# Moving the opening work of a state-space block between VectorE, GpSimd and ScalarE, and reordering the first feed-forward products

## The chip, the core and the metric

The kernel runs on one core of a Trainium2 chip. The metric is the device time of one launch in microseconds (us). TensorE (PE) multiplies and writes PSUM; VectorE (DVE), ScalarE (ACT) and GpSimd (POOL) do the elementwise work; SyncE (SP) issues the DMA transfers. Each engine works through its own list in order, and the lists are tied together by semaphores.

## The reference, cut to what matters

```python
def reference(u, W_in, conv_w, conv_b, dt_bias, A_log, D, norm_w, W_out, W_up, W_gate, W_down):
    x = u                                                  # (2, 2048, 512)
    x = _layernorm(x + attn(x, ...))
    x = _layernorm(x + ffn(x, ternary(W_up), ternary(W_gate), ternary(W_down)))
    return x

def attn(u):
    zxbcdt = einsum('bld,ed->ble', u, W_in)                # z, x, B, C, dt
    dt = softplus(zxbcdt[..., -8:] + dt_bias)
    xBC = silu(causal_conv4(xBC, conv_w, conv_b))
    dA = dt * A;  cum = cumsum(dA)                         # decays within chunks of the sequence
    y = within-chunk product (C B^T * decay) (x dt)  +  C * carried state * exp(cum)  +  x * D
    yg = y * silu(z)
    return einsum('ble,de->bld', yg * rsqrt(mean(yg^2) + eps) * norm_w, W_out)

def ternary(w):                                            # scale = mean(|W|)
    return clip(round(w / scale), -1, 1) * scale

def ffn(x):
    return einsum(silu(x Wu^T) * (x Wg^T), Wd)
```

## The kernel before

The 4096 tokens go in 8 blocks of 512 (`NB`), each block as 8 heads in four pairs (`p` = 0 to 3). Then the feed-forward part runs over the same 8 blocks in 8 slices (`q`) each; its up and gate products are done by seven products per slice instead of eight (`product`, `FACTORS`). Every weight and activation is used as a float16 high part and a float16 low part (`w_hi`, `w_lo`, `split_u`, `x_high`, `x_low`).

What a block does: `head_tile` multiplies one head's x or z columns (12 matmuls into one of three ring banks); `conv_in`, `conv`, `conv_tanh`, `silu` turn the x tile into `x_ch`; `z_tanh`, `z_gate` the z tile into `z_ch`; `cb_tile`, `cb_conv`, `cb_silu` make B and C (`b_ch`, `c_ch`) of the next block; `dt_first`, `dt_second`, `dt_ln`, `dt_third` its step sizes `dts` and `da`. `turn_x` transposes x, `x_dt` scales it, `decays` and `within` make the masked decay matrix `seg`, `states` and `state_update` the chunk states, and `outputs` the result. `skip` adds x times D into `y_ch`, `gate` multiplies by z into `yg`, `gated` and `y_low` split that, `chunk_out` multiplies by W_out. A ring bank is given to the next tile only when its x, z or B/C has been read (`ring_room`).

The order on each engine is written out by hand. Block 0 begins with a straight list (pair 1 of block 0), and `step(0, 0)` goes on with pairs 2 and 3. Into this opening is woven what is done once:

- The input weight comes in six pieces (`PIECES`); ACT makes the high part, DVE the low part. Piece 3 (columns of heads 2 and 3) is split by DVE in two halves (`w_lo_head(2)`, `w_lo_head(3)`), the last piece (heads 6 and 7) by `w_lo(5)`. Where the raw piece 5 lay, `y_hi` is written later, so the first `gated` of block 0 waits for `w_lo(5)`.
- W_out comes in two halves through the buffer `rows`. For each, POOL scales it by the norm weight (`wout_scale`), ACT makes the high part (`wout_hi`), POOL the low part (`wout_low`).
- For the ternary scales, 24 tiles of the feed-forward weights pass through two buffers of `quant`: ACT sums the magnitudes of the even ones, DVE of the odd ones (`magnitude(i)`). `load_abs(i)` waits until tile `i - 2` is summed. All of SP's transfers stand in one queue of issues: one that waits holds up all behind it.

`load_cum(n, par, p)` of SP brings the cumulative decays of a pair and waits for the `decays` that read the buffer before (`relu_ok`).

## Time and profile before

| | us |
|---|---|
| median of 3 runs | 1405.49 |
| lowest and highest | 1405.03, 1407.62 |
| the profiled execution | 1405.99 |
| its span, first to last instruction | 1404.2 |
| PE busy in the span | 1362.4 |
| DVE, ACT, POOL busy in the span | 1070.9, 802.1, 649.9 |
| mean granted TensorE clock | 0.993 |

PE is busy 97% of the span, so a time is won or lost where PE sits idle, or where its clock is granted at half. How to read it: the table of waits names who ended PE's idle stretches; the timeline of one engine gives start and length of each instruction, merged when like ones follow each other, with the idle time ahead of it in brackets.

### The profile page before, as it was taken

The page shows a single profiled execution, that of the slowest core. Times are in us where ns is not written, and L with a number is a line of the kernel's source. Part 1 is how long each engine was busy: PE and PEld are TensorE (multiplying, and loading weights), DVE is VectorE, ACT ScalarE, POOL GpSimd, SP SyncE. Part 2 cuts the span into 40 slices and gives each one's busy share as a digit, 9 for nine tenths or more (in the row PEclk, how much of TensorE's full clock was granted, in tenths as well). Part 3 has the DMA queues.
Part 4 walks back from the last instruction along what each step waited for, and adds up shares of the span by engine and source line. Part 5 has one row for each costly group of instructions (what it writes and reads, how often), then busy time and mean ns, then how long its engine had stood idle before and what let it go on. Part 6 is the DMA issues. An engine that isn't in the chain of part 4 may idle for free.

```text
span 1404.2 us, 27260 instructions
## 1 busy us (share of the span) xinstructions
PE 1362.4 (97%) x9574; PEld 888.9 (63%) x9574; DVE 1070.9 (76%) x1848; ACT 802.1 (57%) x1593; POOL 649.9 (46%) x628
## 2 busy tenths in 40 slices
PE   8899999999999999999999999999999999999998
PEld 4455555555555555556556777777777777777774
DVE  7887877886877879878775887767776767777775
ACT  6686574773856828748565555555455545545441
POOL 0574264673663736625355544434343434434331
PEclk9899999999999999999999999999999999999999
DMA  8436334263342532424325130111101010110002
GB/s 258 160 125 212 127 106 105 80 171 87 105 128 84 164 108 84 143 91 136 124 87 196 61 106 16 47 45 46 34 28 61 31 63 16 59 33 31 31 24 68
DMA packets 101342, 129.16 MB, mean 92 GB/s; under 512 B 40401, under 2 KB 61265, under 8 KB 100049
## 3 DMA queue, kind: packets, MB, share of 16 engines
q1 hardware_dynamic: 101200, 127.35, 29.3%
q8 instruction: 80, 1.31, 0.4%
q14 instruction: 62, 0.50, 0.1%
HBM read 99.93 MB, written 27.39 MB: 91 GB/s over the span
## 4 chain that ended last, share of the span: by engine, by line
PE 60%; issue 13%; DVE 12%; ACT 8%; POOL 6%; DMA 1%; ACTq 0%; POOLq 0%; SPq 0%; DVEq 0%
PE ring L1110 15%; PE p_turn L1090 8%; PE p_y L1090 7%; PE ring L873 7%; PE p_seg L1090 6%; PE p_st L1090 5%; PE ring L902 5%; DVE acc L1806 2%; ACT p_seg L1333 2%; ACT xdt L1324 2%; PE p_y L946 2%; PE p_y L954 2%; DVE seg L1904 1%; POOL sq_sum L1634 1%; DVE st L1918 1%
## 5 line engine op out<-in xcount | busy, mean ns | idle before, releaser
L873 PE MATMUL ring<-u_split,weights 128*128 128x512 f16 x1620 | 376.2, 382 | 2.1 <-DVE x_ch L1811 1.9
L873 PEld LDWEIGHTS ring<-u_split,weights 128*128 128x128 f16 x1620 | 155.6, 99 | 172.2 <-issue 8.0
L1717 POOL TENSOR_TENSOR xdt<-xdt 128x512 f32<-128x512 f32 x64 | 100.2, 1566 | 351.8 <-DVE xdt L2160 351.8
L1806 DVE SCALAR_TENSOR_TENSOR acc<-ring,taps,acc 128x511 f32<-128x511 f32 (+2 forms) x192 | 143.7, 749 | 4.5
L902 PE MATMUL ring<-w_out,raw 128*128 128x512 f16 x672 | 147.1, 379 | 0.0
L1324 ACT ACTIVATE xdt<-p_turn,dts 128x128 f32<-128x128 f32 x256 | 73.0, 376 | 84.9 <-PE p_turn L926 84.9
L1626 POOL TENSOR_TENSOR raw<-yg,raw 128x512 f16<-128x512 f32 x64 | 78.7, 1230 | 79.2 <-ACT raw L1354 78.6
L902 PEld LDWEIGHTS ring<-w_out,raw 128*128 128x128 f16 x672 | 65.7, 98 | 77.8
L1621 POOL TENSOR_TENSOR yg<-y_ch,z_ch 128x512 f32<-128x512 f32 x64 | 81.9, 1280 | 44.1 <-DVE y_ch L1926 44.1
L1333 ACT ACTIVATE p_seg<-cum_rows,cum 128x128 f32<-128x128 f32 x256 | 80.8, 388 | 6.2 <-DVE seg L1904 6.2
L1277 ACT ACTIVATE ring<-acc 128x512 f32<-128x512 f32 x64 | 38.5, 602 | 80.0 <-DVE acc L1806 79.6
L946 PE MATMUL p_y<-seg,xdt 128*128 128x128 f32 x512 | 69.9, 281 | 14.7 <-DVE seg L1904 14.2
L946 PEld LDWEIGHTS p_y<-seg,xdt 128*128 128x128 f32 x512 | 64.2, 191 | 24.4 <-DVE seg L1904 20.1
L1597 POOL TENSOR_TENSOR rstd<-var_e,exponent 128x1 f32<-128x1 f32 x32 | 20.4, 638 | 125.6 <-DVE var_e L1948 125.6
L1634 POOL TENSOR_TENSOR sq_sum<-sq_sum,sq 128x512 f32<-128x512 f32 x56 | 71.1, 1270 | 0.0
L1522 ACT ACTIVATE cum_g<-c_dec,tanh_scale 128x512 f32<-128x512 f32 x32 | 23.1, 722 | 77.6 <-DVE b_dec L2152 77.6
L1522 ACT ACTIVATE cum_g<-b_dec,tanh_scale 128x512 f32<-128x512 f32 x32 | 23.1, 722 | 71.7 <-DVE c_dec L2152 71.2
L1904 DVE TENSOR_TENSOR seg<-p_seg,cb_mask 128x512 f32<-128x512 f32 x64 | 43.9, 686 | 22.1 <-ACT p_seg L1337 22.0
L2152 DVE TENSOR_TENSOR xdt<-grow,p_turn 128x512 f32<-128x512 f32 x64 | 44.0, 687 | 17.1 <-ACT grow L1513 11.5
L1811 DVE SCALAR_TENSOR_TENSOR x_ch<-ring,acc 128x512 f32<-128x512 f32 x64 | 44.1, 689 | 15.8 <-ACT ring L1277 14.9
L2152 DVE TENSOR_TENSOR c_dec<-cum_g,p_turn 128x512 f32<-128x512 f32 x32 | 22.0, 688 | 44.1 <-PE p_turn L1090 44.1
L1522 ACT ACTIVATE grow<-xdt,tanh_scale 128x512 f32<-128x512 f32 x64 | 46.0, 719 | 14.5 <-DVE xdt L2152 13.9
(420 smaller groups left out, 3367.7 us busy)
## 6 DMA issues: line engine op xcount, KB each, us to landing
cum_rows<-cum_dram SPq DMA_DIRECT2D x64, 256.0 KB, 4.1
quant<-in_w_ffn SPq DMA_DIRECT2D x24, 512.0 KB, 4.4
quant<-in_w_ffn SPq DMA_DIRECT2D x48, 256.0 KB, 4.1
cum_g<-cum_dram SPq DMA_DIRECT2D x64, 128.0 KB, 4.4
rows<-in_u_tok SPq DMA_DIRECT2D x32, 256.0 KB, 3.7
x_dram<-rows SPq DMA_DIRECT2D x32, 256.0 KB, 2.0
tern_ug<-quant SPq DMA_DIRECT2D x32, 256.0 KB, 3.5
u_raw<-in_u_t SPq DMA_DIRECT2D x7, 1024.0 KB, 8.4
```

The source lines that it names most:

```text
L873: mm = pe.matmul(bank_k[:, :], w_in[:, ws, k, col:col + P], us[:, par, k * T:(k + 1) * T], start=(i == 0), stop=(i == 3 * KD - 1))
L902: mm = pe.matmul(ring[b][:, :], ys[:, h, c * P:(c + 1) * P], w_out[:, ws, h, :], start=(h == 0 and ys is y_hi and ws == 0), stop=(h == H - ...
L946: pe.matmul(p_y[q][:, c * P:(c + 1) * P], xdt[:, q, c, :], seg[:, q, c, :], start=(c == 0), stop=False, skip_group_check=True)
L1090: mm = pe.matmul(bank_j[:, w * 256:(w + 1) * 256], factor(weight, w, k, q), xs[par][i][:, k, :], start=(first and w == 0 and k == 0 and xs ...
L1110: mm = pe.matmul(p_down[c % 2][:, :], hidden_tile(par, m, low)[:, c * P:(c + 1) * P], t_down(m), start=(e == 0 and m == 0 and not low), st ...
L1324: ins = act.activation(xdt[:, q, c, :], p_turn[:, c * P:(c + 1) * P], ACT.Copy, scale=dts[:, owner, c, h:h + 1])
L1333: ins = act.activation(p_seg[:, c * P:(c + 1) * P], cum_b[:, (2 * p - 2 + q) % 4, c, :], ACT.Relu, bias=cum[:, owner, h, c:c + 1], scale=-1.0)
L1522: act.activation(th[second], up, ACT.Tanh, scale=tanh_scale[:, 0:1]).then_inc(tanh_ok, 1)
L1621: pool.tensor_tensor(yg[:, q, :], y_ch[:, q, :], z_ch[:, k % 4, :], ALU.mult).then_inc(yg_ok, 1)
L1634: pool.tensor_tensor(sq_sum[:, :], sq_sum[:, :], sq[:, q, :], ALU.add).then_inc(sqsum_ok, 1)
L1717: pool.tensor_tensor(tile_[:, 1, :, :], tile_[:, 0, :, :], tile_[:, 1, :, :], ALU.mult).then_inc(hid_ok, 1)
L1806: dve.scalar_tensor_tensor(acc[:, buf, k + 1:T], own[:, 0:T - 1 - k], taps[:, h, 2 - k:3 - k], acc[:, buf, k + 1:T], ALU.mult, ALU.add).th ...
```

## The change

Seven moves, five of them around the first two blocks and two at the feed-forward part:

1. Piece 3 of the input weight is split by POOL, not DVE. Each half is two instructions there (a scaling in place, then a subtraction); they stand first in POOL's list. PE waits for them by `w_half_ok`, and SP's first `load_abs` too.
2. `cb_silu` makes B before C, and `turn_b` waits for B alone; `cb` waits for all three. This holds in all blocks.
3. In pair 2 of block 0 DVE takes `skip` (both heads) and the carry in front of `cb_conv` and `dt_second` of block 1, then `within` of both heads and the state updates in front of the next convolution. `w_lo(5)` comes after `silu(4)`, and `magnitude(3)` behind `silu(5)`, next to `magnitude(5)`. On ACT `cb_tanh` stands ahead of `decays` of the second head.
4. The second half of W_out (`wout_hi(1)`, `wout_low(1)`) and ACT's `magnitude(8)` move from pair 3 of block 0 to pair 0 of block 1.
5. SP issues tiles 10 and 11 behind `load_cum(1, ·, 1)` and `load_u(2)` of block 1.
6. Opening of the feed-forward part: PE does product 5 ahead of product 6; ACT reads product 7 ahead of the last two `gated`.
7. The last block's `rms` on POOL and its `residual(NB-1, 0)` on DVE stand earlier in slice 2.

```diff
 def head_weights(h):
-    return 1 + h if h < 2 else 2 + h // 2
+    return 2 + h if h < 2 else 2 + h // 2
...
+        def act_rows(n, p, when):
+            if when == 2 and is_at(n, 0) and p == 3:
+                return None
+            return 8 if when == 0 and is_at(n, 1) and p == 0 else abs_rows(n, p, when)
...
@@ SP, step(0, 0), pair 0
-                        sp.wait_ge(w_lo_ok, 4)
+                        sp.wait_ge(w_lo_ok, 3)
+                        sp.wait_ge(w_half_ok, 2)
...
                     if is_at(n, 0) and p == 3:
                         load_abs(8)
                         load_abs(9)
+                    if is_at(n, 1) and p == 0:
+                        load_cum(n, par, 1)
+                        load_u(2)
                         load_abs(10)
                         load_abs(11)
-                    if is_at(n, 1) and p == 0:
                         load_abs(12)
                         load_abs(13)
-                        load_cum(n, par, 1)
-                        load_u(2)
...
@@ PE
             def turn_b(n, use):
-                wait_apart(pe, bc_ok, n * 3 + 3, passed["pe"])
+                wait_apart(pe, bc_ok, n * 3 + 1, passed["pe"])
...
             def cb(n, par, use):
                 pe.wait_ge(turn_free, use)
+                wait_apart(pe, bc_ok, n * 3 + 3, passed["pe"])
...
             product(0, 0, 0, 1, True)
+            pe.wait_ge(turn_free, turn_use(NB, "x01") + 1)
+            product(0, 0, 0, 5, True)
             pe.wait_ge(s1_ok, 1)
             product(0, 0, 0, 6, False)
-            pe.wait_ge(turn_free, turn_use(NB, "x01") + 1)
-            product(0, 0, 0, 5, True)
             outputs(NB, 0, 0)
...
@@ ACT, step
                     if state_slot(n, p):
                         x_dt(n, par, p, 1)
+                        if is_at(n, 0) and p == 2:
+                            cb_tanh(1, ring[ring_bank("cb", 0)])
                         decays(n, par, p, 1)
-                    if is_at(n, 0) and p == 2:
-                        cb_tanh(1, ring[ring_bank("cb", 0)])
...
+                    if is_at(n, 1) and p == 0:
+                        wout_hi(1)
                     if not end:
                         conv_tanh(n, 2 * p + 1)
...
-                    if is_at(n, 0) and p == 3:
-                        wout_hi(1)
...
             gated(NB, 0, 1)
+            chain_read(0, 0, u3, prod[7], u3_ok, c21_ok)
             act.wait_ge(scales_ok, 3)
             gated(NB, 1, 0)
             gated(NB, 1, 1)
...
@@ POOL
+            def w_lo_head(h):
+                own = raw_piece(3)[:, :, 2 * P * (h - 2):2 * P * (h - 1)]
+                pool.wait_ge(w_hi_ok, 4)
+                pool.tensor_scalar(own, own, SW, None, ALU.mult).then_inc(w_mul_ok, 1)
+                pool.wait_ge(w_mul_ok, h - 1)
+                pool.tensor_tensor(w_in[:, 1, :, 2 * P * h:2 * P * (h + 1)], own, w_in[:, 0, :, 2 * P * h:2 * P * (h + 1)],
+                                   ALU.subtract).then_inc(w_half_ok, 1)
...
+            w_lo_head(2)
+            w_lo_head(3)
             b_decay(0, 0, 0, turn_use(0, "b0"))
...
-                    if is_at(n, 0):
-                        wout_scale(1) if p == 2 else wout_low(1)
+                    if is_at(n, 0) and p == 2:
+                        wout_scale(1)
                     if p == 0 and more(n) and not is_at(n, 0):
                         corrections(n + 1, 1 - par)
+                    if is_at(n, 1) and p == 0:
+                        wout_low(1)
...
@@ DVE
             cum_turned(0, turn_use(0, "cumt0"))
-            w_lo_head(2, w_half_ok)
             cb_silu(0, 0, p_y[0])
             z_gate(0, 0)
-            w_lo_head(3, w_lo_ok)
             b_read(0, 0, turn_use(0, "b0"))
...
             w_lo(4)
             magnitude(1)
-            w_lo(5)
-            cb_conv(1, 1, ring[ring_bank("cb", 0)])
-            dt_second(1)
...
+                    if first and p == 2:
+                        cb_conv(1, 1, ring[ring_bank("cb", 0)])
+                        dt_second(1)
...
                     if first and p == 2:
                         cb_silu(1, 1, ring[ring_bank("cb", 0)])
-                    if abs_rows(n, p, 0) is not None:
+                        within(n, par, p, 1)
+                        for c in range(C - 1):
+                            state_update(n, par, p, c)
+                    elif abs_rows(n, p, 0) is not None:
                         magnitude(abs_rows(n, p, 0) + 1)
...
-                    if state_slot(n, p):
+                    if first and p == 2:
+                        w_lo(5)
+                    elif state_slot(n, p):
...
+                    if first and p == 2:
+                        magnitude(abs_rows(n, p, 0) + 1)
                     if abs_rows(n, p, 2) is not None:
                         magnitude(abs_rows(n, p, 2) + 1)
...
+                    if attention_rest(t, q) == 0:
+                        residual(NB - 1, 0, p_down[0])
                     if before:
                         summed(m, k, "c12", u2, u2_ok, 5, ALU.add)
```

Three places show what the moves make of the lists. In the names, `rows` holds the raw weight piece 3, `quant` a magnitude tile, `x_ch`, `z_ch` and `y_ch` are `silu`, `z_gate` and `skip`.

DVE at the end of the straight list's first third (block 0, behind the first `silu`), before:

```order
L1811 SCALAR_TENSOR_TENSOR x_ch<-ring,acc 128x512 [waits th_ok]
L1888 COPY cum_t<-p_turn 32x128 [waits turn_full]
L1781 SCALAR_TENSOR_TENSOR weights<-rows,weights 128x4x256 [waits w_hi_ok]
L1830 SCALAR_TENSOR_TENSOR c_ch<-p_y,acc 64x512 [waits thc_ok]
L1830 SCALAR_TENSOR_TENSOR c_ch<-p_y,acc 64x512
L1832 SCALAR_TENSOR_TENSOR b_ch<-p_y,acc 64x512
L1839 SCALAR_TENSOR_TENSOR z_ch<-thz,ring 128x512 [waits thz_ok]
L1781 SCALAR_TENSOR_TENSOR weights<-rows,weights 128x4x256 [waits w_hi_ok]
```

POOL behind its constants, now:

```order
L1677 TENSOR_SCALAR rows<-rows 128x4x256 [waits w_hi_ok,made]
L1679 TENSOR_TENSOR weights<-rows,weights 128x4x256 [waits w_mul_ok]
L1677 TENSOR_SCALAR rows<-rows 128x4x256 [waits w_hi_ok]
L1679 TENSOR_TENSOR weights<-rows,weights 128x4x256 [waits w_mul_ok]
L1617 TENSOR_TENSOR b_dec<-b_tok,dec 128x4x64 [waits dec_ok,turn_free]
```

The two splits have left DVE, and four POOL instructions now run from the moment the fourth high part is made.

DVE at the end of pair 2 of block 0, before:

```order
L1879 COPY cum<-p_turn 128x32 [waits turn_full]
L1882 TENSOR_TENSOR darg<-p_turn,cum 128x32 [waits dec_ok,cum_ok]
L1811 SCALAR_TENSOR_TENSOR x_ch<-ring,acc 128x512 [waits th_ok]
L1786 TENSOR_REDUCE abs_sum<-quant 128x1 [waits abs_in1]
L1926 SCALAR_TENSOR_TENSOR y_ch<-x_ch,d_skip,p_y 128x512 [waits yg_ok,y_full]
L1926 SCALAR_TENSOR_TENSOR y_ch<-x_ch,d_skip,p_y 128x512 [waits yg_ok]
```

and now:

```order
L1896 COPY cum<-p_turn 128x32 [waits turn_full]
L1899 TENSOR_TENSOR darg<-p_turn,cum 128x32 [waits dec_ok,cum_ok]
L1828 SCALAR_TENSOR_TENSOR x_ch<-ring,acc 128x512 [waits th_ok]
L1803 TENSOR_REDUCE abs_sum<-quant 128x1 [waits abs_in1] x2
L1943 SCALAR_TENSOR_TENSOR y_ch<-x_ch,d_skip,p_y 128x512 [waits yg_ok,y_full]
L1943 SCALAR_TENSOR_TENSOR y_ch<-x_ch,d_skip,p_y 128x512 [waits yg_ok]
```

Two magnitudes (tiles 3 and 5) stand there in a row where one stood; both use the same buffer.

SP from the magnitude tiles of pair 3 of block 0 on, before:

```order
L589 DMA quant<-in_w_ffn 128x1024 [waits abs_ok0]
L589 DMA quant<-in_w_ffn 128x1024 [waits abs_ok1]
L597 DMA cum_dram<-cum_t 32x128 [waits turn_free]
L607 DMA cum_rows<-cum_dram 128x512 [waits grow_ok,relu_ok,cumt_out]
L608 DMA cum_g<-cum_dram 64x512
L607 DMA cum_rows<-cum_dram 128x512
L608 DMA cum_g<-cum_dram 64x512
L589 DMA quant<-in_w_ffn 128x1024 [waits abs_ok0]
L589 DMA quant<-in_w_ffn 128x1024 [waits abs_ok1]
L607 DMA cum_rows<-cum_dram 128x512 [waits grow_ok,relu_ok]
L608 DMA cum_g<-cum_dram 64x512
```

and now:

```order
L614 DMA cum_rows<-cum_dram 128x512 [waits grow_ok,relu_ok]
L615 DMA cum_g<-cum_dram 64x512
L614 DMA cum_rows<-cum_dram 128x512
L615 DMA cum_g<-cum_dram 64x512
L600 DMA u_raw<-in_u_t 128x2048 [waits u_lo_ok]
L596 DMA quant<-in_w_ffn 128x1024 [waits abs_ok0]
L596 DMA quant<-in_w_ffn 128x1024 [waits abs_ok1]
L596 DMA quant<-in_w_ffn 128x1024 [waits abs_ok0]
L596 DMA quant<-in_w_ffn 128x1024 [waits abs_ok1]
```

Tiles 10 and 11 were issued ahead of the store of block 1's decays; now they are issued behind the second group of its loads and behind the next block's u.

## Rows read from the trace of the kernel before

**Rows 1.** Page, part 1: busy us (share) and instructions of each engine.
```profile
PE 1362.4 (97%) x9574; PEld 888.9 (63%) x9574; DVE 1070.9 (76%) x1848; ACT 802.1 (57%) x1593; POOL 649.9 (46%) x628
```
**Rows 2.** Waits of PE, 0 to 200 us: us in total, times, longest.
```profile
PE p_y L946 <- DVE seg L1904: 5.2, 6, 1.9
PE p_turn L911 <- DVE b_ch L1832: 3.7, 2, 3.1
PE p_st L936 <- DVE carry L1918: 2.6, 1, 2.6
```
**Rows 3.** Timeline of PE: start us, length us, line, instruction [idle before, releaser].
```profile
65.03 4.84 PE L873 MATMUL ring<-u_split,weights 128*128 128x512 f16 x12
...
97.77 0.63 PE L926 MATMUL p_turn<-ident,x_ch 128*128 128x128 f32 x4 [1.48 <-ACT xdt L1324]
...
114.47 0.60 PE L926 MATMUL p_turn<-ident,x_ch 128*128 128x128 f32 x4
```
**Rows 4.** Timeline of DVE, 18 to 23 us.
```profile
18.12 0.19 DVE L1873 TENSOR_TENSOR da<-dts,a_neg 128x32 f32<-128x32 f32 x1
18.30 0.16 DVE L1802 TENSOR_TENSOR acc<-acc,corr 128x3 f32<-128x3 f32 x1
...
22.29 1.20 DVE L1781 SCALAR_TENSOR_TENSOR weights<-rows,weights 128x1024 f16<-128x1024 f32 x1
```
**Rows 5.** Timeline of ACT: the high part of piece 3.
```profile
15.71 1.90 ACT L1249 ACTIVATE weights<-rows 128x2048 f16<-128x2048 f32 x1
```
**Rows 6.** One line of DVE: duration in ns, min/median/max, first and last start.
```profile
L1802 DVE TENSOR_TENSOR acc<-acc,corr x64: 151/678/1271, 18.3 to 733.0; 128x3 f32<-128x3 f32 x64
```
**Rows 7.** POOL: one timeline row, then durations (ns) of two lines.
```profile
1.92 0.95 POOL L1588 MEMSET carry<- 128x1024 f32 x1
...
L1669 POOL TENSOR_TENSOR rows<-rows,norm_s x8: 1041/1043/1046, 39.6 to 77.9; 128x512 f32<-128x512 f32 x8
...
L1676 POOL TENSOR_TENSOR w_out<-rows,w_out x8: 1152/1159/3199, 48.0 to 96.4; 128x512 f16<-128x512 f32 x8
```
**Rows 8.** Timeline of DVE, 53 to 87 us.
```profile
53.57 1.11 DVE L1818 TENSOR_TENSOR acc<-acc,corr 128x3 f32<-128x3 f32 x1
...
75.35 0.69 DVE L1811 SCALAR_TENSOR_TENSOR x_ch<-ring,acc 128x512 f32<-128x512 f32 x1 [0.33 <-ACT ring L1277]
75.95 1.21 DVE L1786 TENSOR_REDUCE abs_sum<-quant 128x1 f32<-128x1024 f32 x1
77.08 1.40 DVE L1926 SCALAR_TENSOR_TENSOR y_ch<-x_ch,d_skip,p_y 128x512 f32<-128x512 f32 x2
...
80.50 0.69 DVE L1904 TENSOR_TENSOR seg<-p_seg,cb_mask 128x512 f32<-128x512 f32 x1 [1.16 <-ACT p_seg L1337]
```
**Rows 9.** Timeline of SP's issues: start, length of the issue.
```profile
108.19 0.38 SPq L607 DMA_DIRECT2D cum_rows<-cum_dram  x1
...
110.23 0.96 SPq L593 DMA_DIRECT2D u_raw<-in_u_t  x1
```
**Rows 10.** DMA issues, 0 to 120 us: KB each, median us from issue to landing.
```profile
quant<-in_w_ffn SPq DMA_DIRECT2D x16, 512.0 KB, 4.7
...
rows<-in_u_tok SPq DMA_DIRECT2D x2, 256.0 KB, 10.1
```
**Rows 11.** Timeline of ACT, 92 to 103 us.
```profile
92.38 2.17 ACT L1254 ACTIVATE w_out<-rows 128x512 f16<-128x512 f32 x4
94.46 1.04 ACT L1258 ACTIVATE quant<-quant 128x1024 f32<-128x1024 f32 x1
...
100.94 1.27 ACT L1333 ACTIVATE p_seg<-cum_rows,cum 128x128 f32<-128x128 f32 x4
```
**Rows 12.** Timeline of PE, the opening of the feed-forward part.
```profile
747.06 1.05 PE L1090 MATMUL ring<-b_tok,weights 128*128 128x256 f16 x8 [0.69 <-ACT cum_g L1513]
...
757.80 1.05 PE L1090 MATMUL p_turn<-c_ch,weights 128*128 128x256 f16 x8 [1.37 <-DVE xdt L2152]
...
776.57 2.76 PE L1147 MATMUL ring<-w_out,raw 128*128 128x512 f16 x12 [0.37 <-DVE rows L1941]
```

35 lines of the change are left out of this document (16 added, 19 removed).

## The prediction, made before the result was known

> **What bounds the kernel now.** I read the page's first part first: PE is busy 97% of the span [rows 1], so only its idle stretches and its half-clock stretches can be won. The table of PE's waits over the first 200 us comes next [rows 2]. The reader should see that the large single waits are two: 2.6 us on the carry behind `skip` (L936), and 3.1 us on B of block 1 (L911). PE's timeline then shows what follows them: a tile of 12 matmuls at 65.03 takes 4.84 us where the same kind takes 2.76 at full clock [rows 3, 12], so PE ran at 1.2 instead of 2.4 GHz there. A third wait, 1.48 us at 97.77, is on ACT. In the rest of the first 130 us PE waits little, but that doesn't mean that DVE and ACT have room: they are nearly as late as PE. Last I read SP's issues and the landing times [rows 9, 10], because the change moves loads.
>
> The sum is made against the profiled execution (span 1404.2, time 1405.99) and its difference is put on the median, 1405.49. A lateness that PE carries into its long run of W_out products at the end of block 1's pair 1 passes to the end, since PE hardly waits after that.
>
> **1. Piece 3 on GpSimd.** DVE loses two instructions of 1.13 us each, start to start (22.29 in [rows 4], and one more like it), 2.3 us, in a stretch where PE waits for DVE. Unhindered that is worth 2.0 us. Now POOL's side. ACT's high part ends at 15.71 + 1.90 = 17.6 [rows 5]. No scaling of 1024 elements by a constant is in the trace. A fill of that size takes 0.95, a two-operand product of 512 takes 1.04, so 2.08 for two of them [rows 7]: the bounds. I take 1.2, near the fill, since only one operand is read. The subtraction is twice 1.16 = 2.3. Both halves are done at 17.6 + 2 × 3.5 = 24.6, the first at 21.1, earlier than DVE made it (22.29 + 1.20), so PE doesn't wait for the weights.
>
> But DVE and POOL hinder each other. The three-element addition of `conv` takes 151 ns alone and up to 1271 [rows 6], and 1.11 at 53.57 [rows 8], when POOL was in the low parts of W_out, one of which took 3.2 instead of 1.16 [rows 7] because DVE's own low part was running. All these DVE instructions read two operands from SBUF. At 18.12 and 18.30 stand two more of that kind, `da` and the first addition of `conv` [rows 4]. POOL's four instructions now start just ahead of them. `da` then waits behind the first subtraction, until 17.6 + 1.2 + 2.3 = 21.1, and the addition behind the second scaling, until 22.3: 4.0 us late, less the 2.3 given back, **+1.7** (with the bounds of the scaling +1.2 to +3.5; without hindrance −2.0). PE meets it as a wait for `da` ahead of `cum_proj` at about 18.4 and for the first `silu` later.
>
> No row shows a DVE instruction as wide as `da` held by POOL, only three-element ones. The Trainium skill, "SBUF — State Buffer", section "Who interferes with whom", says that a DVE instruction with two SBUF inputs and a GpSimd one that reads SBUF exclude each other for a whole instruction, whichever starts first. By that rule `da` is held and the sum is the one below; by the rows alone the opening could as well give −2.0, the first rival.
>
> **2. Pair 2 of block 0.** With `skip` and the carry first, `states` needs no wait, and B comes after ACT's earlier `cb_tanh`: both waits of [rows 2] go, and most of the half clock. Behind them DVE is next: `w_lo(5)` now stands in front of `dt_third` and of ACT's first `gated`, so `cum_proj` waits about 5 us for `da` of block 1. What is left, from DVE's order, is that `silu(5)` (75.35 before [rows 8]) comes about 2.0 earlier: one magnitude of 1.13 has moved behind it, and DVE's own idle time is some 1.7 shorter, less 0.8 that it waits for ACT.
>
> That gain is spent at once. `magnitude(3)` now ends at 73.9 + 1.1 = 75.0, and only then may SP issue tile 5, for the same buffer. The median from issue to landing is 4.7 [rows 10], so `magnitude(5)` runs 79.7 to 80.9, and `skip` behind it starts at 80.9 instead of 77.08 [rows 8]: **+3.8**. If the tile landed at once it would be −0.9; at the 10.1 that two other tiles took it would be +9. I take the median of its own kind. The load of the second half of W_out stands behind tile 5 in SP's queue; POOL's `wout_scale(1)` and the gates behind it come later too, which holds `z_gate(6)`: 0.5 more. Against it DVE had 1.16 idle at 80.50 [rows 8]. So `outputs` of pair 3 is 3.1 late.
>
> **3. Pair 0 of block 1.** ACT no longer does W_out (2.17) and tile 8 (1.04) at 92.38 [rows 11], which made the 1.48 wait [rows 3]. Its `z_tanh(7)` ran 2.4 behind its tile, so of the 3.1 it keeps 0.7; a tile at half clock after PE's wait costs up to 2.1 more (4.84 less 2.76), I take 1.0. `decays` of pair 0, which end at 100.94 + 1.27 = 102.2 [rows 11], are then **+1.7** late on top of item 1.
>
> **4. Tiles 10 and 11.** `load_cum(1, ·, 1)` waits for just those `decays`. Its four issues and that of u take 3.0 (108.19 to 110.23, plus 0.96 [rows 9]), so tile 10 is issued 3.0 behind them, and lands 4.7 to 10.1 later [rows 10] (its own median, and that of two transfers issued right behind the same five). I take 6.5, between them but nearer to its kind: landed at 9.5. ACT is there at 3.9 and waits 5.6; DVE waits as long for tile 11. Then ACT has `magnitude(10)` 1.1, `conv_in` and `gated` 1.7, W_out 2.1, `conv_tanh` 0.5, the wait for tile 12 (issued at 10.6, landed 15.3), `magnitude(12)` and the `z_tanh` and `growth` in front of `x_dt` 3.1: 18.4 behind `decays`. Before, PE transposed that head at 114.47 [rows 3], 12.3 behind them. **+6.1** (+4.4 with 4.7, +9.7 with 10.1). PE stands idle 5 to 6 us there, ahead of `turn_x` and the z tile of head 2.
>
> **5. B first** in all other blocks: `cb_silu` runs a pair ahead of `turn_b`, under PE's W_out products. 0. **W_out later**: its products come 15 us after the new place. 0.
>
> **6. Feed-forward opening.** Product 5 needs only `x_dt` of the second head, long done, and hides the 0.69 wait; ACT's read of product 7 ahead of two `gated` that wait for POOL ends the 1.37 wait; `rms` and `residual` earlier end the 0.37 wait [rows 12]. **−2.4**; if `outputs` or the W_out product behind them is late instead, −1.
>
> Sum: 1.7 + 1.7 + 6.1 − 2.4 = +7.1, less 0.5 for two short waits for DVE and POOL in block 1 that are there anyway: **+6.6, 1412**.
>
> **The rivals.** *No hindrance in the opening*: POOL starts a little later or DVE's small instructions slip between. Item 1 is −2.0: 1405.5 + 2.9 = 1408.4. For it: the row of a held instruction is of another shape. Against: POOL has four in a row. *The cover holds, and it gets faster*: the mechanism is the loads. If tile 5 and tile 11 land before DVE and PE need them, that is, in under 1 us and under 1.5 us beyond DVE's own work, item 2 keeps −0.9, item 3 adds the 1.48, item 6 the 2.4, and with item 1 between −2.0 and +1.7 it is 1398.7 to 1402.4; I take 1401. For it: PE has one tile of slack in its ring at each place. Against: a round trip through SP can't be shorter than a landing, and 4.7 is the median. *All prices at their upper end*: scaling 2.08 and landings of 10.1: +3.5 + 1.7 + 9.7 − 2.4 = +12.5, 1418. *The change doesn't do what it says* is no case: the lists show the moves.
>
> **The numbers.** Forecast 0.50, no hindrance 0.23, faster 0.15, upper end 0.10, the rest elsewhere. A measurement of this kernel can tell about 0.2% from no change, 2.8 us. Under 1402.7 lies most of the faster case: 0.15. From there to 1408.3: half of the second case and the forecast's low edge, 0.20. Above: 0.65. The range that leaves out 2 in 10 is 1403 to 1417: below it most of the faster case, above it most of the upper end.
>
> **What would show it.** Item 1: DVE's `da` and first `conv` addition at 1 us or more each, PE idle about 3 us at 18.4. Item 2: no wait at `states` and `turn_b` of pair 2, about 5 us at `cum_proj`, and two magnitudes on DVE with a wait for DMA of about 4 us between. Item 4: waits of ACT and DVE for `quant` DMAs near 110 us, and PE idle ahead of 120. Item 6: no idle time at the three places. Wrong would be: `da` at 0.2 us, tiles landing within 3 us, or PE busy through 115 to 123 us.

## The result, and the profile of the changed kernel

| | before | changed |
|---|---|---|
| median | 1405.49 us | 1411.82 us |
| all runs | 1404.87 to 1407.62 | 1410.27 to 1412.98 |
| profiled execution: span | 1404.2 | 1411.2 |

The ratio is 1.0041 (95% interval 1.0031 to 1.0052): the changed kernel is slower by 0.3 to 0.5%, beyond the 0.2% that can be told from no change. The forecast was 1412.0.

PE does as much as before, in a longer span (part 1 of the page: busy us, share, instructions; before it was [rows 1]):

```profile
PE 1361.0 (96%) x9574; PEld 887.5 (63%) x9574; DVE 1070.2 (76%) x1846; ACT 801.9 (57%) x1593; POOL 657.9 (47%) x632
```

So idle time was added. PE's waits from 0 to 200 us (us in total, times, longest), to be laid beside [rows 2]:

```profile
PE p_turn L935 <- ACT xdt L1333: 6.6, 1, 6.6
PE p_y L955 <- DVE seg L1921: 6.5, 4, 2.3
PE p_turn L853 <- DVE da L1890: 5.3, 3, 4.2
```

The wait of 2.6 for the carry is gone, that of 3.1 for B is down to 1.5. In their place stand 4.2 for `da` of block 1 and one of 6.6 for ACT, at a place where PE had no idle time before. Where they lie is seen on PE's timeline (start, length; in brackets the idle time before it and what ended it):

```profile
71.14 0.60 PE L853 MATMUL p_turn<-da,tri_ones 128*128 128x32 f32 x2 [4.17 <-DVE da L1890]
71.98 5.28 PE L881 MATMUL ring<-u_split,weights 128*128 128x512 f16 x12
...
124.18 1.09 PE L935 MATMUL p_turn<-ident,x_ch 128*128 128x128 f32 x4 [6.57 <-ACT xdt L1333]
125.06 4.36 PE L881 MATMUL ring<-u_split,weights 128*128 128x512 f16 x12
```

Behind both waits the tile of 12 matmuls takes 5.28 and 4.36 us instead of 2.76. The granted clock is 0.51 of full over the first of these tiles and 0.63 over the second: after it stood idle, PE ran at 1.2 instead of 2.4 GHz for the whole of the one and most of the other. That is the second part of what these waits cost. The same transposition, `turn_x` of that head, was at 114.47 before [rows 3], so PE is 9.7 us late at that point.

ACT (108.2 to 115.4 us) and DVE (109.6 to 116.7) both stood still for a transfer, and earlier DVE alone. The first two lines are the earlier place, the last two the later one:

```profile
79.46 1.22 DVE L1803 TENSOR_REDUCE abs_sum<-quant 128x1 f32<-128x1024 f32 x1 [3.56 <-DMA quant<-in_w_ffn]
80.59 1.40 DVE L1943 SCALAR_TENSOR_TENSOR y_ch<-x_ch,d_skip,p_y 128x512 f32<-128x512 f32 x2
...
115.43 1.06 ACT L1267 ACTIVATE quant<-quant 128x1024 f32<-128x1024 f32 x1 [7.24 <-DMA quant<-in_w_ffn]
...
116.66 1.22 DVE L1803 TENSOR_REDUCE abs_sum<-quant 128x1 f32<-128x1024 f32 x1 [7.08 <-DMA quant<-in_w_ffn]
```

The feed-forward opening, in PE's timeline, has none of the waits of 0.69 and 1.37 of [rows 12]. From the start of the W_out product ahead of it to the start of the one behind it are 16.7 us, before 18.8 (741.60 to 760.43):

```profile
751.13 2.76 PE L1156 MATMUL ring<-w_out,raw 128*128 128x512 f16 x12
...
767.86 2.76 PE L1156 MATMUL ring<-w_out,raw 128*128 128x512 f16 x12
```

**The lateness, place by place** (start of the same instruction, changed less before; from the two timelines). The forecast is the sum of the prediction's terms up to that place, the opening's +1.7 included:

| place | before | changed | late by | forecast |
|---|---|---|---|---|
| `outputs` of pair 0, block 0 | 47.12 | 46.13 | -1.0 | +1.7 |
| `skip` of pair 2 | 77.08 | 80.59 | +3.5 | +5.5 |
| `outputs` of pair 3, the carried part | 88.52 | 91.91 | +3.4 | +4.8 |
| end of `decays`, pair 0 of block 1 | 102.21 | 104.48 | +2.3 | +3.4 |
| `turn_x` behind tile 10 | 114.47 | 124.18 | +9.7 | +9.5 |
| first W_out products of block 1 | 129.26 | 139.36 | +10.1 | |
| W_out product ahead of the feed-forward part | 738.40 | 747.93 | +9.5 | |
| W_out product behind its opening | 760.43 | 767.86 | +7.4 | |
| end | | | +7.0 | +6.6 |

The table compares two single executions. How much the first places move between executions of the same code is seen from the traces of all the runs below: `outputs` of pair 0 starts between 45.49 and 47.71 in the ten traces with the changed opening, 46.55 on average, and at 46.45, 46.72 and 47.12 in the three with the old one. So the -1.0 of the first row is within that spread; on average the two openings are 0.2 apart.

### The profile page after: what moved, and what is told of

Same layout as the page of the kernel before. It is cut to its first block, busy times and chain, and to the rows that moved or that the text cites. A ratio compares the mean times of both kernels' runs of the same rounds, so it can differ in the third digit from the quotient of the medians.

```text
span 1411.2 us, 27276 instructions
## 1 busy us (share of the span) xinstructions
PE 1361.0 (96%) x9574; PEld 887.5 (63%) x9574; DVE 1070.2 (76%) x1846; ACT 801.9 (57%) x1593; POOL 657.9 (47%) x632
## 4 chain that ended last, share of the span: by engine, by line
PE 59%; issue 13%; DVE 12%; ACT 8%; POOL 5%; DMA 2%; SPq 0%; ACTq 0%; POOLq 0%; DVEq 0%
PE ring L1119 15%; PE p_turn L1099 7%; PE ring L881 7%; PE p_y L1099 7%; PE p_seg L1099 5%; PE p_st L1099 5%; PE ring L910 4%; DVE acc L1823 3%; ACT p_seg L1342 2%; ACT xdt L1333 2%; PE p_y L955 2%; PE p_y L963 2%; DVE seg L1921 1%; DVE st L1935 1%; POOL sq_sum L1645 1%
```

## The experiments

"Measured" gives the median, then the ratio to executions of the kernel before made together with that run (their medians lie between 1405.4 and 1405.9), with its 95% interval. Two kernels whose intervals overlap are not told apart by their times; then the traces are compared, and the text says so. `W_out at` is the start of the first W_out products of block 1 (before 129.26, changed 139.36), which sums up the first blocks without the later stretches. It is read from one execution, so a difference of about 1 us can be chance.

### Run 1: tiles 8, 10 and 11 early again

```diff
 def act_rows(n, p, when):
-    if when == 2 and is_at(n, 0) and p == 3:
-        return None
-    return 8 if when == 0 and is_at(n, 1) and p == 0 else abs_rows(n, p, when)
+    return abs_rows(n, p, when)
...
                     if is_at(n, 0) and p == 3:
                         load_abs(8)
                         load_abs(9)
+                        load_abs(10)
+                        load_abs(11)
                     if is_at(n, 1) and p == 0:
                         load_cum(n, par, 1)
                         load_u(2)
-                        load_abs(10)
-                        load_abs(11)
                         load_abs(12)
```

> Changed kernel with tiles 10 and 11 issued in pair 3 of block 0 again and ACT's magnitude of tile 8 back there; the second half of W_out stays late. Theory: PE's 6.6 us ahead of turn_x at 124.2 exist only because tile 10 is issued 3 us behind decays and lands 7 us later. Then ACT's wait of 7.2 and DVE's of 7.1 vanish, ACT's 1.1 for tile 8 is covered by its wait for z_tanh(7), and turn_x comes 12.3 to 13 behind decays instead of 19.7: about -7.4, 1404.4. Rival: the W_out high parts (2.2 us) that now stand in front of conv_tanh on ACT make most of it, together with POOL's low parts; then 3 us or more of the idle time stays and the time is 1407 to 1409.

Measured: 1409.83 us, 1.0030 [1.0017, 1.0042]; W_out at 135.97. Not 1404: the time lies just above the rival's range. The wait for tile 10 is gone, but ACT now waits for tile 12, and PE keeps 2.53 of 6.57. ACT's timeline:

```profile
111.54 2.18 ACT L1261 ACTIVATE w_out<-rows 128x512 f16<-128x512 f32 x4
114.77 0.60 ACT L1284 ACTIVATE ring<-acc 128x512 f32<-128x512 f32 x1 [1.05 <-DVE acc L1821]
117.53 1.06 ACT L1265 ACTIVATE quant<-quant 128x1024 f32<-128x1024 f32 x1 [2.16 <-DMA quant<-in_w_ffn]
```

W_out's high parts stand in front of `conv_tanh` in this run too, and ACT has to wait for DVE (1.05) behind them anyway, so they hold nothing up: the rival's mechanism falls. What stayed is again a tile issued behind `load_cum` and u: SP issued tile 12 at 109.97, and it landed 7.5 later. (The wait of 2.53 had no half clock behind it; the tile that follows took 2.75.)

### Run 2: the order of the loads alone

```diff
                     if is_at(n, 1) and p == 0:
+                        load_abs(10)
+                        load_abs(11)
                         load_cum(n, par, 1)
                         load_u(2)
-                        load_abs(10)
-                        load_abs(11)
                         load_abs(12)
```

> Changed kernel, only SP's order in pair 0 of block 1: tiles 10 and 11 ahead of the four loads of cum and of u. Theory (order of issue): tile 10 is issued right behind ACT's magnitude of tile 8, at 106.2 instead of about 107.7, and no 1 MB transfer is ahead of it, so it lands after 4.7: 110.9, ACT waits 2.8 instead of 7.2; -4.4, 1407.4. Rival (the transfers share the engines whatever the order): it lands 7.5 behind its issue again, 113.7, only -1.6, 1410.2.

Measured: 1413.06 us, 1.0051 [1.0038, 1.0065]; slower than either forecast, and by its time not told apart from the changed kernel. The profiled execution was the slowest of the five, 1417.31, and the other four lie between 1412.94 and 1413.24; W_out at 142.88 is of that one. ACT's timeline shows both tiles, with the wait ahead of each:

```profile
114.35 1.06 ACT L1267 ACTIVATE quant<-quant 128x1024 f32<-128x1024 f32 x1 [1.61 <-DMA quant<-in_w_ffn]
...
124.08 1.06 ACT L1267 ACTIVATE quant<-quant 128x1024 f32<-128x1024 f32 x1 [4.17 <-DMA quant<-in_w_ffn]
```

and SP's timeline (start and length of the issues) when they were issued:

```profile
110.72 0.81 SPq L596 DMA_DIRECT2D quant<-in_w_ffn  x2
...
113.66 0.58 SPq L600 DMA_DIRECT2D u_raw<-in_u_t  x1
115.52 1.70 SPq L596 DMA_DIRECT2D quant<-in_w_ffn  x2
```

Tile 10, ahead of u, was there 3.6 us after its issue; tile 12, behind u, 8.6 us after. So a tile is late because of what is in front of it, and not because all these loads are under way at the same time: the wait moved from one tile to the next (1.6 + 4.2 in place of 7.2). The edit itself brings 1.3 us, near the rival's 1.6: the turn ahead of tile 10's place comes 4.5 later than in the changed kernel (118.96 against 114.42), the one behind it 3.2 (127.41 against 124.18). Those 4.5 have nothing to do with the edit, since they lie in front of it. 1.6 are there at `outputs` of pair 0 already (47.71 against 46.13). The other 2.9 are half clock in pair 3 of block 0, behind a wait for `seg` of 2.94 us (2.26 in the changed kernel):

```profile
97.68 4.58 PE L881 MATMUL ring<-u_split,weights 128*128 128x512 f16 x12
```

The granted clock is 0.50 from 94 to 98 us here and 0.98 there, and the same tile took 2.76 there. That explains the profiled execution. Why the other four, at 1413, show nothing of the 1.3 to 1.6 us that the edit should bring stays open.

### Run 3: tile 3's magnitude early again

```diff
                         for c in range(C - 1):
                             state_update(n, par, p, c)
+                        magnitude(abs_rows(n, p, 0) + 1)
                     elif abs_rows(n, p, 0) is not None:
...
-                    if first and p == 2:
-                        magnitude(abs_rows(n, p, 0) + 1)
```

> Changed kernel, only DVE's magnitude of tile 3 back in front of conv of head 4, in pair 2 of block 0. Theory: DVE's wait of 3.56 us for tile 5 goes because SP can issue the tile 12 us earlier; skip starts at 77.0 to 77.5 instead of 80.6, the second half of W_out lands in time and the 0.97 wait at z_gate(6) goes too; the lateness passes unshrunk through pair 0 of block 1, since load_cum there waits for decays: -3.5, 1408.3. Rival: the 1.2 us ahead of conv pass on through silu(4), w_lo(5) and ACT's gated to the cum products, and half of the gain is lost: -1.5 to -2, 1410.

Measured: 1410.99 us, 1.0034 [1.0022, 1.0046]; W_out at 137.32, 2.0 earlier. By the times it can't be told from the changed kernel, and the profiled execution, 1413.51, is the slowest of its six; so what follows rests on the first 140 us of the traces. DVE's wait for tile 5 is gone and `skip` starts 3.6 earlier, as the theory said, but DVE then waits for ACT:

```profile
76.94 1.40 DVE L1943 SCALAR_TENSOR_TENSOR y_ch<-x_ch,d_skip,p_y 128x512 f32<-128x512 f32 x2
79.07 0.69 DVE L1856 SCALAR_TENSOR_TENSOR z_ch<-thz,ring 128x512 f32<-128x512 f32 x1 [0.48 <-ACT thz L1302]
82.36 0.69 DVE L1921 TENSOR_TENSOR seg<-p_seg,cb_mask 128x512 f32<-128x512 f32 x1 [2.60 <-ACT p_seg L1346]
```

ACT's `decays` are that late because PE's turns are, and those because `da` of block 1 now comes later still. PE's timeline:

```profile
72.25 0.61 PE L853 MATMUL p_turn<-da,tri_ones 128*128 128x32 f32 x2 [6.99 <-DVE da L1890]
...
73.10 5.31 PE L881 MATMUL ring<-u_split,weights 128*128 128x512 f16 x12
```

`outputs` of pair 3 come only 1.5 earlier (90.38). The rival had the mechanism, and the size by the traces: two paths run side by side here, the tile's and that of `da`, 1.5 to 2 us apart. And the wait for tile 11 stays, 7.49 on DVE.

### Run 4: both

The edits are those of runs 1 and 3.

> The edits of the first and the third run together. Theory: the two waits are independent and one behind the other on the path: -7.4 - 3.5 = -10.9, about 1401, under the kernel before (the opening and the feed-forward step together give 3.5 of that). Rival: the two share a cover (SP's queue of tiles is one chain, and W_out's second half loads earlier in both), so the second gives under 1.5: 1403 or more.

Measured: 1406.37 us, 0.9998 [0.9989, 1.0007]; W_out at 132.86. The kernel before is reached, 1401 is not. The rival falls: the two alone move the W_out products by 3.4 and 2.0, together by 6.5. (The time does lie where the rival put it, 1403 or more, but not by its mechanism.) The size is missed by the wait that was left, now larger since all else is earlier. ACT:

```profile
109.27 0.60 ACT L1284 ACTIVATE ring<-acc 128x512 f32<-128x512 f32 x1
114.69 1.06 ACT L1265 ACTIVATE quant<-quant 128x1024 f32<-128x1024 f32 x1 [4.82 <-DMA quant<-in_w_ffn]
```

SP issued u at 105.94 and tile 12 at 106.57; the tile landed 8.1 later. PE waits 4.30 for it.

### Run 5: every tile ahead of u

The kernel of run 4 with this:

```diff
                     if is_at(n, 1) and p == 0:
+                        load_abs(12)
+                        load_abs(13)
                         load_cum(n, par, 1)
                         load_u(2)
-                        load_abs(12)
-                        load_abs(13)
```

> As the fourth run, and tiles 12 and 13 ahead of the four loads of cum and the load of u again. In the runs so far the wait did not go, it moved to tile 12: issued right behind u at 106.6 it landed 8.1 later (114.7), where a tile issued ahead of u landed 3.6 later. Theory (the transfer of u, 1 MB, in front of a tile is what makes it late): ACT's wait of 4.8 at tile 12 and PE's 4.3 go, the half clock behind goes (1.5): -5 to -5.5, 1401. Rival: load_cum, now behind tile 12 and so behind ACT's magnitude of tile 10, makes growth and decays of pair 1 late instead (by 3 us or more), 1405.

Measured: 1401.97 us, 0.9964 [0.9950, 0.9979]; W_out at 126.99. SP and ACT:

```profile
104.77 1.70 SPq L594 DMA_DIRECT2D quant<-in_w_ffn  x2
...
108.60 0.74 SPq L598 DMA_DIRECT2D u_raw<-in_u_t  x1
```

```profile
109.10 1.05 ACT L1265 ACTIVATE quant<-quant 128x1024 f32<-128x1024 f32 x1
```

Tile 12 is issued at 104.8 and has landed when ACT takes it at 109.1, without a wait; PE transposes at 112.85 with no idle time in front, at full clock. `load_cum` is issued at 106.57, in run 4 at 103.76, and nothing waits for it: the rival falls. This is the changed kernel with its tile loads and the magnitudes of tiles 3 and 8 where they were before, and it is faster than both: between the loss of 0.41% and the gain of 0.36% stand only those.

### Run 6: the feed-forward opening alone

The kernel before with the last part of the change: product 5 ahead of product 6 on PE, ACT's read of product 7 ahead of the last `gated`, `rms` ahead of `hidden` on POOL, `residual(NB - 1, 0)` ahead of `summed` on DVE. PE's lines:

```diff
             product(0, 0, 0, 1, True)
+            pe.wait_ge(turn_free, turn_use(NB, "x01") + 1)
+            product(0, 0, 0, 5, True)
             pe.wait_ge(s1_ok, 1)
             product(0, 0, 0, 6, False)
-            pe.wait_ge(turn_free, turn_use(NB, "x01") + 1)
-            product(0, 0, 0, 5, True)
```

> The kernel before with only the changes of the first feed-forward step. Theory: the waits of 0.7, 1.4 and 0.4 go as they went in the changed kernel, -2.4, 1403.2. Rival: the lateness that the W_out products and DVE carry comes back behind them (residual and hidden of the first step meet DVE later), less than 1 us is left, 1405.

Measured: 1402.90 us, 0.9982 [0.9970, 0.9994]. PE:

```profile
744.71 1.05 PE L1090 MATMUL ring<-xs_more,weights 128*128 128x256 f16 x8
745.59 1.04 PE L1090 MATMUL p_turn<-u_raw,weights 128*128 128x256 f16 x8
746.47 1.04 PE L1090 MATMUL ring<-b_tok,weights 128*128 128x256 f16 x8
```

Product 5 (`p_turn`) runs in the place of the 0.69 wait. From the W_out product at 740.99 to the one at 757.72 it is 16.7 us instead of 18.8. The W_out product that had the wait of 0.37 in front of it starts 15.6 behind that one (773.32), before 16.1 (776.57 [rows 12]). The theory holds: -2.1 and -0.5, and the interval of the time goes from -0.9 to -4.2 us.

### Run 7: the opening alone

The kernel before with `w_lo_head` on POOL, ahead of `b_decay`, as in the change, and nothing else. POOL's lines, then DVE's.

```diff
+            w_lo_head(2)
+            w_lo_head(3)
             b_decay(0, 0, 0, turn_use(0, "b0"))
...
-            w_lo_head(2, w_half_ok)
             cb_silu(0, 0, p_y[0])
             z_gate(0, 0)
-            w_lo_head(3, w_lo_ok)
```

> The kernel before with only the opening: GpSimd makes the low part of piece 3. Theory (from the changed kernel's trace): da and the first conv addition are not held, outputs of pair 0 come 1.0 earlier, but pair 2 of block 0 is bound by DVE's own order and keeps it: -1.0, 1404.5. Rival (the prediction's term): the two engines hinder each other, +1.7, 1407.2. Second rival: the gain is lost at the carry wait in pair 2 because POOL's later W_out parts hold it, 0.

Measured: 1405.38 us, 0.9997 [0.9985, 1.0009]. `outputs` of pair 0 come 0.4 earlier than in the kernel before (46.68), W_out at 128.19; both are within what differs between executions, since run 6, with the old opening, has them at 46.45 and 127.92. The forecast's +1.7 (ratio 1.0012) is just outside the interval, the -1.0 inside, and so is nothing at all. DVE's timeline shows that `da` and the addition behind it are not held:

```profile
17.56 0.96 DVE L1876 SCALAR_TENSOR_TENSOR dts<-dt_x,dt_s 128x32 f32<-128x32 f32 x1
18.55 0.19 DVE L1879 TENSOR_TENSOR da<-dts,a_neg 128x32 f32<-128x32 f32 x1
18.66 0.15 DVE L1808 TENSOR_TENSOR acc<-acc,corr 128x3 f32<-128x3 f32 x1
```

while on POOL the scaling ran all the time:

```profile
17.44 2.78 POOL L1668 TENSOR_SCALAR rows<-rows 128x1024 f32<-128x1024 f32 x1 [14.57 <-ACT weights L1251]
20.30 2.13 POOL L1670 TENSOR_TENSOR weights<-rows,weights 128x1024 f16<-128x1024 f32 x1
```

### Run 8: step sizes ahead of the last weight piece

The first lines are ACT's, the others DVE's.

```diff
                         conv_tanh(n, 2 * p)
+                    if p == 2 and is_at(n, 0):
+                        dt_ln(1)
                     if gate_slot(n, p):
                         gated(n, p, 0)
...
-                    if first and p == 2:
-                        w_lo(5)
-                    elif state_slot(n, p):
+                    if state_slot(n, p) and not (first and p == 2):
...
                         dt_third(n + 1, 1 - par)
+                    if first and p == 2:
+                        w_lo(5)
```

> As the fifth run, and in pair 2 of block 0 ACT's dt_ln stands ahead of gated and DVE's dt_third ahead of w_lo(5). Theory: PE's wait of 5.3 for da of block 1 is made of w_lo(5) 2.3, DVE's own wait for dt_l 2.5 and the short operations; both go, da comes at about 66.5 when PE gets there, the half clock behind it (2.1) goes too; DVE's 2.5 us idle time is won, so skip of pair 2 comes 2.5 earlier: -2.5 behind the fifth run, about 1398.5. Rival: w_lo(5) now holds ACT's gated, conv_in(5) and the turn of x by 2 us, so that silu(5) does not move: no gain, 1401.

Measured: 1400.88 us, 0.9955 [0.9939, 0.9970]: against run 5, on which this edit stands, the times don't tell. In the trace PE waits 2.82 for `da` instead of 6.99, but `skip` comes no earlier when the opening is taken out: from `outputs` of pair 0 to `skip` it is 29.65 us (45.49 to 75.14), in run 5 29.57 (47.09 to 76.66). DVE does `w_lo(5)` at once and then waits for ACT, which waits for just that `w_lo(5)` in front of `conv_in`:

```profile
65.88 0.19 DVE L1890 TENSOR_TENSOR da<-dts,a_neg 128x32 f32<-128x32 f32 x1
65.99 2.29 DVE L1798 SCALAR_TENSOR_TENSOR weights<-raw,weights 128x2048 f16<-128x2048 f32 x1
70.22 0.16 DVE L1819 TENSOR_TENSOR acc<-acc,corr 128x3 f32<-128x3 f32 x1 [1.94 <-ACT acc L1279]
```

The rival is right for `skip`. What is won is on PE: 78.8 us from `outputs` of pair 0 to the W_out products (124.30) instead of 79.9, so 1.1, of one execution each.

### Run 9: `conv_in` ahead of `gated` too

```diff
                     if p == 2 and is_at(n, 0):
                         dt_ln(1)
+                        conv_in(n, 2 * p + 1)
...
-                    if not end:
+                    if not end and not (is_at(n, 0) and p == 2):
                         conv_in(n, 2 * p + 1)
```

> As the eighth run, and in pair 2 of block 0 ACT's conv_in of head 5 stands ahead of gated too. In the eighth run ACT stood 3.2 us at gated for w_lo(5), and DVE, done with w_lo(5) at 68.2, stood 1.9 for the acc of head 5 behind it. Theory: the 1.9 goes, silu(5) and skip come 1.9 earlier, PE's 2.2 ahead of the turn of head 5 and the half clock behind it (1.7) go: -2 to -3 behind the eighth run, 1398 to 1399. Rival: PE's lateness comes back from ACT (gated later, decays of pair 3 later) and nothing is won: 1401.

Measured: 1399.14 us, 0.9952 [0.9939, 0.9965], the fastest of all by its median, but not told apart from run 8. The 1.94 is gone, and most of it stands one step on, where ACT's `conv_tanh` is still behind the two `gated`:

```profile
71.14 0.16 DVE L1820 TENSOR_TENSOR acc<-acc,corr 128x3 f32<-128x3 f32 x1
...
75.45 0.69 DVE L1829 SCALAR_TENSOR_TENSOR x_ch<-ring,acc 128x512 f32<-128x512 f32 x1 [1.46 <-ACT ring L1284]
```

From `da` (68.82) to `skip` (77.18) it takes 8.4 us, in run 8 9.3: 0.9 gained of the 1.9. It doesn't reach the W_out products, 80.2 behind `outputs` of pair 0 (127.40), 1.4 more than in run 8. In this execution `dt_w` and `dt_m` were both held (1.32 and 1.20) and in run 8 only `dt_m`; even so the two are level at `outputs` of pair 3 (88.79 and 87.02, both 41.5 to 41.6 behind those of pair 0). The 1.4 go behind that, in waits for `seg` of up to 1.29, and why is open. In the traces it is nearer to the rival.

### Run 10: the ninth, with piece 3 on DVE

The edit is the opening of the change taken back.

> As the ninth run, but DVE makes piece 3's low parts again, as in the kernel before. Theory: the opening's 1.0 us is a shift of everything behind it and shows in full once pair 2 has no larger wait: +1.0, 1399.5 where the ninth is 1398.5. Rival: it is absorbed, as it seemed in the seventh run (0.5 under the kernel before): same within 0.5.

Measured: 1400.07 us, 0.9964 [0.9951, 0.9977]. The median is 0.9 above run 9's, the theory's size, but the intervals overlap, and the profiled executions go the other way (W_out at 125.49 against 127.40; PE waits 0.24 for B here, 1.46 in run 9). By runs 7 and 10 no worth of the opening is shown either way: run 7's interval goes from -2.1 to +1.3 us. Its sign in the forecast, +1.7, has no support in either.

### Run 11: the ninth, with W_out early

ACT's high parts, and POOL's low parts in the same way.

```diff
-                    if is_at(n, 1) and p == 0:
-                        wout_hi(1)
...
+                    if is_at(n, 0) and p == 3:
+                        wout_hi(1)
```

> As the ninth run, but the second half of W_out gets its high part on ACT at the end of pair 3 of block 0 and its low part on POOL there, as in the kernel before. Theory: ACT's z_tanh(7) is then 2.2 us late, growth and x_dt of pair 0 of block 1 behind it, PE waits 1.5 for the turn of x as it did before: +1.5, 1400. Rival: with DVE and ACT earlier there is slack, and the 2.2 us only move from pair 0 of block 1 to pair 3: same within 0.5.

Measured: 1403.23 us, 0.9981 [0.9972, 0.9991], slower than run 9 (whose interval ends at 0.9965). The wait of the kernel before [rows 3, 1.48 at 97.77] is back:

```profile
96.38 0.63 PE L933 MATMUL p_turn<-ident,x_ch 128*128 128x128 f32 x4 [1.60 <-ACT xdt L1331]
```

So moving W_out's second half pays, by the medians 4 us. The profiled executions show less of it. The W_out products start at 127.37 here and at 127.40 in run 9, where `dt_w` was held and here not; from `outputs` of pair 3 on, which leaves that out, it is 40.0 us here and 38.6 in run 9, so 1.4, about the wait. The rest of the 4 is not accounted for.

### Run 12: the scaling with two operands

The kernel of run 7 with this (and the filling of `w_scale` ahead of it, among POOL's constants):

```diff
-pool.tensor_scalar(own, own, SW, None, ALU.mult)
+pool.tensor_tensor(own, own, w_scale[:, :, :].broadcast_to([P, KD, 2 * P]), ALU.mult)
```

> The seventh run's kernel (the kernel before and the opening alone) with GpSimd's scaling of 1024 elements done as a product with a second operand (a column of 64, broadcast) instead of a product with a constant. It tells what held DVE: in the changed kernel a product with a constant ran 2.8 us and held DVE's dts for 0.8 only, while da and the first conv addition passed under it. Theory (an instruction that reads two operands holds DVE's two-operand instructions for its whole length, one with a constant doesn't): scaling 2.1 us, dts held until it ends at 17.4 + 2.1 = 19.6, the next one until the subtraction ends at 21.7, PE waits for da 1 us or more, outputs of pair 0 0.5 to 2 us later than in the seventh run, time +0.5 to +1.5. Rival (the hold depends on who starts first, not on the number of operands): dts 1.0 again and da free, the scaling is 0.7 shorter, time as the seventh, 1405.4.

Measured: 1408.87 us, 1.0022 [1.0011, 1.0033]. POOL, then DVE:

```profile
17.96 1.89 POOL L1670 TENSOR_TENSOR rows<-rows,w_scale 128x1024 f32<-128x1024 f32 x1 [15.05 <-ACT weights L1252]
19.94 2.18 POOL L1672 TENSOR_TENSOR weights<-rows,weights 128x1024 f16<-128x1024 f32 x1
```

```profile
18.11 1.79 DVE L1878 SCALAR_TENSOR_TENSOR dts<-dt_x,dt_s 128x32 f32<-128x32 f32 x1
19.94 0.19 DVE L1881 TENSOR_TENSOR da<-dts,a_neg 128x32 f32<-128x32 f32 x1
20.05 2.08 DVE L1810 TENSOR_TENSOR acc<-acc,corr 128x3 f32<-128x3 f32 x1
```

`dts` ends at 19.90, when the scaling ends (19.85), and the addition at 22.13, when the subtraction ends (22.12). So each of the two is held to the end of a POOL instruction, and the addition is ready within 0.2 us of what the prediction said, 22.3. It is not the prediction's picture in full: `dts` is the one that is held, and `da` (19.94 to 20.13) slips between scaling and subtraction, where the prediction had it wait until 21.1. PE waits 1.77 us for `da`, and the tile behind it takes 4.44. The W_out products come 1.1 later than in run 7 (129.28), within what was expected, but no later than in the kernel before (129.26). The medians are 3.5 apart, more than the +0.5 to +1.5 expected; in the profiled executions most of the rest stands in block 2, where here a tile at 170.93 took 4.71 us at the lower clock and in run 7 the same one 2.75. The hold that the prediction described is that of this kernel; in the changed kernel, whose scaling has one operand, it ends early.

## Why the prediction was right

The time was met within 0.2 us, and the two waits that make the kernel slower were forecast in their place, for their cause and near their size. That it was met so closely is luck: in the two traces the opening was off by -2.7, the stretch from pair 2 to `decays` of block 1 by +1.6, the tiles by +1.7, and these nearly cancelled. Of the -2.7, about 0.8 is this pair of executions; by the averages over the traces the opening is off by -1.9.

**1. Piece 3 on GpSimd: wrong, the +1.7 and the price.** The prediction's own sign of being wrong here, "`da` at 0.2 us", came true: `da` took 0.19, and it was `dts` that was held, 0.97. Two things failed. The price of the scaling: taken 1.2, bounds 0.95 to 2.08, measured 2.78 and 2.76. The subtraction, forecast 2.3, took 2.13 and 2.12. And the hold: the step "`da` then waits behind the first subtraction, until 21.1" failed because the constant scaling left DVE a free window. In all ten traces with it DVE is held from its start for 1.05 to 1.1 us and then free. In run 7 `dts` ends at 18.52, 1.08 behind the start at 17.44; in run 9, where the scaling started only at 18.97, the addition at 19.48 ends at 20.02, 1.05 behind it. `da` and the first addition slipped between the scaling's first microsecond and the subtraction. Only the second `conv` addition met a subtraction (1.27). The first rival, "DVE's small instructions slip between", was right about the mechanism, and too high about its worth: -1.0 in the changed kernel, -0.4 in run 7, -0.2 on average over the traces, where -2.0 was forecast. Run 12 has the forecast's hold, and `outputs` of pair 0 is 0.6 later in it than in the kernel before (47.74), not 1.7. The Trainium skill, "SBUF — State Buffer", section "Who interferes with whom", lets a DVE instruction with two SBUF inputs and a GpSimd one that reads SBUF exclude each other for a whole instruction; run 12's trace agrees for instructions of two operands, to 0.05 us, and with a constant scaling the traces agree for the first 1.1 of 2.8 us only, so for that form the measurement decides.

**2. Pair 2: right mechanism, 0.7 short, out of two misses.** `skip` came at 80.59 (80.9 in the working), DVE's wait for tile 5 was 3.56 (about 4), PE's for `da` 4.17 (about 5), the wait at `states` is gone. But the 80.9 was on top of +1.7 of the opening; seen from the opening `skip` is 4.5 late, not 3.8. `silu(5)` (74.08), forecast 2.0 earlier than before, came only 0.3 earlier as seen from the opening, so tile 5 was issued 1.9 later than forecast (75.92); and it landed 3.5 behind its issue and not 4.7, which gave 1.2 back. DVE's own idle time, taken as 1.7 shorter, did not shrink: 2.43 ahead of `cb_silu` before, 2.48 ahead of `dt_third` now, where ACT's `dt_ln` stands behind the `gated` that waits for `w_lo(5)`. And one more step failed: the wait at `turn_b` did not go, it is 1.46. The profile gives the reason, DVE's `dt_w` and `dt_m`, ahead of `b_ch`:

```profile
53.93 1.33 DVE L1873 TENSOR_SCALAR dt_w<-dt_e 128x32 f32<-128x32 f32 x1
55.29 1.20 DVE L1875 TENSOR_SCALAR dt_m<-dt_w 128x32 f32<-128x32 f32 x1
```

They ran under these two of POOL:

```profile
53.95 1.27 POOL L1624 TENSOR_TENSOR c_dec<-grow,c_ch 128x512 f32<-128x512 f32 x1
55.17 1.28 POOL L1632 TENSOR_TENSOR yg<-y_ch,z_ch 128x512 f32<-128x512 f32 x1
```

They took 0.17 and 0.18 in the kernel before; now they fall under POOL's `c_decay` (to 55.22) and `gate` (to 56.45) and end with them. Where `dt_w` escaped, in runs 5, 8 and 10, PE's wait for B is 0.23 to 0.24 us. I had counted DVE's moves and not what they move under. Run 3 shows that the tile was not alone on the path: with it gone, `da` decides 1.5 to 2 us lower.

**3. Pair 0 of block 1: right by itself.** Half clock was put at 1.0 and cost 1.1 (late by 3.4 at `outputs`, by 4.5 at the z tile of head 7, 94.96 against 90.50). ACT's margin was put at 2.4, and 2.2 went until the end of `decays`. That `decays` were 2.3 late with an opening 1.0 early, 3.3 apart where 1.7 was forecast, came with what step 2 handed on.

**4. Tiles 10 and 11: right mechanism, too small.** The tile landed 7.8 behind its issue (issued 107.60, taken by ACT at 115.43; 6.5 was forecast, bounds 4.7 to 10.1), ACT waited 7.24 (5.6 forecast), and a half-clock tile of 4.36 followed, which was not in the sum: +7.8 at the W_out products instead of +6.1. Runs 1, 2, 4 and 5 settle that the order in the queue is the cause: a tile issued behind `load_cum` and the 1 MB of u took 7.5 to 8.6 us, one issued ahead of them 3.4 to 3.6, and with all tiles ahead of them (run 5) the loss is gone. The prediction named both loads, and no run parts them. Two tiles of the changed kernel do, in part: tile 4, issued right behind four loads of `load_cum` with no u among them (at 60.71), and tile 10, behind four such loads and u (at 107.60):

```profile
quant<-in_w_ffn SPq DMA_DIRECT2D x1, 512.0 KB, 5.4
quant<-in_w_ffn SPq DMA_DIRECT2D x1, 512.0 KB, 7.8
```

So both seem to cost: about 1.9 us and 2.4 more beyond the 3.5 of a tile with nothing in front. That is an estimate from these two tiles; in the other traces tile 4 took 4.8 to 6.3.

**5. B first, W_out later.** The first was not tested alone. Of the second, item 5 put the later W_out products at 0, and nothing waits for them in the trace; what ACT gains by it was in item 3, the 2.4 of margin that kept most of the lateness from PE. Run 11, where the tiles come in time, shows the same gain as the 1.60 wait that returns without it.

**6. Feed-forward opening: right.** Forecast -2.4, measured -2.1 and -0.5 in the traces, and 0.06 to 0.30% in run 6.

"The cover holds" was wrong for this kernel, since both tiles came late, and the right picture of what this change could be: with the loads back in place (run 5) it is 1402, where that rival had said 1401.

## What to carry to other kernels

When work is moved between engines, follow the buffer each moved instruction frees: here one magnitude that came 10 us later (64.39 before, 74.69 now) held SP's whole queue, and with it tile 5 and W_out's second half (issued at 66.02 before, at 76.30 now). A small load that is needed soon belongs ahead of a large one in the queue, whatever its own wait seems to cost. And price a stall together with the half clock behind it: here it added 2.5 us to a wait of 4.2, and 1.6 to one of 6.6, while behind the waits of 2.53 in run 1 and 1.60 in run 11 the tile took 2.75 and nothing was added. Last, read a total that fits step by step: here three misses of 1.6 to 2.7 us hid in a sum that was right to 0.2.
